# Edge messages with Wn2 padded to 128 columns, row groups for 20 quads, and edge attributes issued by ScalarE

## What is computed

```
gates    = (ssp(edge_state @ We1 + be1) @ We2 + be2) * soft_cutoff(distance)
h        = ssp(node_state[edges] (source and destination, 128 features) @ Wn1 + bn1) @ Wn2 + bn2
messages = h * gates
sums     = zeros.at[destination].add(messages)
x        = layernorm(x + x + ssp(sums @ Ws1 + bs1) @ Ws2 + bs2)
```

## Time and profile before

| | before |
|---|---|
| median of 3 runs | 1972.11 us (1970.78 to 1973.83) |
| the profiled execution | 1974.56 us, span 1972.8 us |
| mean granted clock of TensorE | 0.900 |
| PE / PEld / ACT busy | 1813.2 / 1389.2 / 1463.7 us |
| POOL / DVE busy | 1474.1 / 1233.8 us |
| HBM read and written | 139.69 and 9.87 MB |

### The profile page before, as it was taken

The page is one execution under the profiler, slowest core; times in us unless marked ns, Lnnn a source line. Parts: engine busy times, 40 slices in busy tenths (PEclk is TensorE's granted clock), DMA queues, the critical chain, the costliest instruction groups (busy, mean ns, idle before and its releaser), DMA issues.

```text
span 1972.8 us, 54212 instructions
## 1 busy us (share of the span) xinstructions
PE 1813.2 (92%) x16249; PEld 1389.2 (70%) x16249; DVE 1233.8 (63%) x3520; ACT 1463.7 (74%) x2593; POOL 1474.1 (75%) x1559
## 2 busy tenths in 40 slices
PE   3998998999999899989999999999999999999988
PEld 2777776777767677767777777777777666777766
DVE  4676765665756564655546666666667565566667
ACT  2586876775758676776768888888888777687877
POOL 7777777777777777777777777777777777777773
PEclk7598988896969896996869999999999998798999
DMA  6344434443444333343333334333333333333332
GB/s 125 77 82 93 94 82 90 79 86 76 82 76 71 76 70 64 70 71 69 67 64 80 78 75 80 76 75 81 73 82 74 72 75 73 68 75 76 72 72 45
DMA packets 238853, 151.26 MB, mean 77 GB/s; under 512 B 41936, under 2 KB 209822, under 8 KB 238746
## 3 DMA queue, kind: packets, MB, share of 16 engines
q0 software_dynamic: 49632, 50.87, 19.3%
q1 hardware_dynamic: 184773, 98.53, 18.6%
q10 hardware_dynamic: 4341, 0.72, 0.3%
HBM read 139.69 MB, written 9.87 MB: 76 GB/s over the span
## 4 chain that ended last, share of the span: by engine, by line
PE 43%; ACT 13%; SPq 13%; issue 11%; DMA 8%; DVE 6%; POOL 4%; DVEq 1%; ACTq 1%
PE ps L763 12%; PE ps L809 11%; PE ps L813 6%; SPq L409 5%; DMA ea<-in_edge_attr_dram 4%; PE ps L724 4%; POOL ga L549 4%; ACT lg L1121 3%; ACT lg L1116 3%; PE ps L701 3%; SPq L391 3%; PE ps L837 3%; DMA ga<-in_x_dram,srcT 2%; DVE hid L1413 2%; DVE hid L1417 2%
## 5 line engine op out<-in xcount | busy, mean ns | idle before, releaser
L549 POOL DMA_INDIRECT ga<-in_x_dram,srcT x1551 | 1473.1, 950 | 473.7 <-issue 437.1
L1108 ACT ACTIVATE lg<-ps,bn1c 128x512 f32<-128x512 f32 x390 | 267.9, 687 | 414.6 <-PE ps L724 409.5
L809 PE MATMUL ps<-wn,hid 128*128 128x64 f32 x3120 | 468.3, 297 | 56.4 <-DVE hid L1417 53.0
L809 PEld LDWEIGHTS ps<-wn,hid 128*128 128x128 f32 x3120 | 412.6, 206 | 90.6 <-DVE hid L1417 75.1
L1413 DVE SCALAR_TENSOR_TENSOR hid<-ps,neg_b,lg 128x512 f32<-128x512 f32 x390 | 292.0, 749 | 245.1 <-ACT lg L1121 240.2
L1116 ACT ACTIVATE lg<-lg 128x768 f32<-128x768 f32 x390 | 336.1, 862 | 0.0
L1121 ACT ACTIVATE lg<-lg 128x768 f32<-128x768 f32 x390 | 332.5, 852 | 0.0
L763 PE MATMUL ps<-xe,wn 64*128 64x256 f32 x1560 | 302.8, 468 | 0.5 <-DMA bw<-b_tab 0.5
L813 PE MATMUL ps<-we,hid 128*128 128x128 f32 x1560 | 284.8, 309 | 0.0
L1070 ACT COPY xe<-ps 128x512 f32<-128x512 f32 x390 | 229.4, 588 | 60.5 <-PE ps L703 59.6
L763 PE MATMUL ps<-ohT,bw 46*128 46x256 f32 x1560 | 259.5, 411 | 0.0
(11 more groups left out here) (173 smaller groups left out, 1634.7 us busy)
## 6 DMA issues: line engine op xcount, KB each, us to landing
ea<-in_edge_attr_dram SPq DMA_DIRECT2D x195, 256.0 KB
stage<-in_x_dram SPq DMA_DIRECT2D x1664, 0.2 KB
ga<-in_x_dram,srcT POOLq DMA_INDIRECT x1551
bw<-b_tab SPq DMA_DIRECT2D x782, 23.0 KB
relb<-rel_tab SPq DMA_DIRECT2D x196, 64.0 KB
b_tab<-share SPq DMA_DIRECT2D x24, 250.0 KB
out_dram<-xs SPq DMA_DIRECT2D x24, 125.0 KB
xs<-in_x_dram SPq DMA_DIRECT2D x5, 500.0 KB
```

Of the source, the lines that this page charges most:

```text
L549: pool.indirect_dma_start(to[:, t % 2, t // 2, :], None, x, bass.IndirectOffsetOnAxis(ap=idx[:, t:t + 1], axis=0)).then_inc(done, inc)
L809: pe.matmul(hg[:, t * D:(t + 1) * D], hid[:, u % 2, t * P:(t + 1) * P], wn2[:, :], start=False, stop=False, skip_group_check=True)
L1108: act.activation(lg[:, u % 2, 0:QUAD].rearrange("p (k e) -> p k e", k=2), z[:, :, 0:PAIR], ACT.Abs, bias=bn1c[:, 0:1])
```

## The change

Three edits. (1) Wn2 is kept in a tile of twice the width whose second half is zero (one more memset at the start). The matmuls of L809, and those of the last quad, move all 128 columns: 64 go to the messages' place of the PSUM bank, 64 zeros are added to the place of the gates. (2) The row quads are each 16th from quad 80, 20 in all; rows are fetched in turns of 16, one for each pair of quads from 22 quads ahead; PE waits for `handed` every 16th quad. (3) ea is issued by ACT: for quads 4 and 5 before its first step, then behind L1121 of each odd quad q for quads q+5 and q+6. The condition, that quad q+2 has been turned, is the same as on SP. SP loads ea for quads 0 to 3 alone.

```diff
-ROWS_EVERY = 24
-ROWS_N = 13
-ROWS_BEFORE = 30
-ROWS_TURN = (12, 8, 12, 12, 8, 12, 12, 8, 12, 12, 8, 12)
-HAND = 8
+ROWS_EVERY = 16
+ROWS_N = 20
+ROWS_BEFORE = 22
+ROWS_TURN = (16,) * 8
+HAND = 16
...
-        wn2 = sb("wn2", [P, D])
+        wn2w = sb("wn2w", [P, 2, D])
+        wn2 = wn2w[:, 0, :]
...
                 load_rel(q, u)
                 load_bw(q, v, firsts)
-                if reached(q, RING):
-                    load_ea(q, u)
                 load_rows(q)
                 hand_rows(q)
...
-                    pe.matmul(hg[:, t * D:(t + 1) * D], hid[:, u % 2, t * P:(t + 1) * P], wn2[:, :],
+                    pe.matmul(hg.rearrange("p (h t d) -> p t h d", h=2, t=4)[:, t, :, :], hid[:, u % 2, t * P:(t + 1) * P], wn2w[:, :, :],
                               start=False, stop=False, skip_group_check=True)
...
+            def load_ea(q, u):
+
+                act.wait_ge(xe_t, q - (RING - 2))
+                issue_ea(act, q, u)
+
             def fast_step(q, u, node=None, share_off=None):
                 if isinstance(q, int) and q == 0:
                     evacuate(0, 0)
                     evacuate(1, 1)
+                    load_ea(RING, 0)
...
                 logs(q, u)
+                if u % 2 == 1:
+                    load_ea(q + RING + 1, (u + 1) % RING)
...
                     logs(q, q % RING)
                     node_step(*node)
+                    if q % 2 == 1 and q + RING + 1 < NQ:
+                        load_ea(q + RING + 1, (q + 1) % RING)
...
+            dve.memset(wn2w[:, 1, :], 0.0)
```

More of the change, by code:

```diff
@@ L317, in general_of, with issue_ea @@
             return eng.value_load(flag_i[0:1, 0:1], min_val=0, max_val=1)
+        def issue_ea(eng, q, u):
+            if isinstance(q, int) and q == NQ - 1:
+                eng.dma_start(ea[0:LP, u, :, :],
+                              edge_attr[q * QUAD:E, :].rearrange("(k p j) d -> p k (j d)", k=2, j=2)).then_inc(s_ea[u], 16)
+            else:
+                two = edge_attr[bass.ds(q * QUAD, 2 * QUAD), :]
+                eng.dma_start(ea[:, u:u + 2, :, :].rearrange("p q k c -> p (q k) c"),
+                              two.rearrange("(m p j) d -> p m (j d)", p=P, j=2)).then_inc(s_ea[u], 16)
         LAST0 = PB // 15 * 15
@@ L368, in load_ea @@
                     sp.wait_ge(xe_t, q - (RING - 2))
[L369 to L375, removed]
+                issue_ea(sp, q, u)
             def load_rel(q, u):
@@ L794, in mid_last @@
                 for t in range(4):
-                    pe.matmul(hg[:, t * D:(t + 1) * D], hid[:, u % 2, t * P:t * P + LP], wn2[:, :],
+                    pe.matmul(hg.rearrange("p (h t d) -> p t h d", h=2, t=4)[:, t, :, :], hid[:, u % 2, t * P:t * P + LP], wn2w[:, :, :],
                               start=False, stop=False, skip_group_check=True)
```

## The result

| | before | after |
|---|---|---|
| median of the runs (us) | 1972.69 (1970.78 to 1977.28, 6 runs) | 2004.6 (1995.45 to 2016.93, 6 runs) |
| ratio, from all runs of both | | 1.0146, 95% interval 1.0119 to 1.0173 |
| profiled execution, its span (us) | 1974.56, 1972.8 | 1995.68, 1993.8 |
| granted clock, mean | 0.90 | 0.932 |

The forecast was 1966.6 us, with a range up to 1998. The kernel got 1.5% slower (the quotient of the two medians alone is 1.0162). The profiled execution is the second shortest of the six, 9 us under the median; all rows of "after" are of it.

The account below looks back on a forecast made before the run. POOL's gathers were taken to bound the kernel, before and after. Span 1972.8 - 7.5 (gathers removed) + 2 (ea's cost at the end) = 1967.3; the same 5.5 us off the median gave 1966.6 us, range 1961 to 1998.

Parts of the forecast that it names:

- What bounds the kernel before: Whole run: POOL's gathers, one each 1.25 us without a break, set the pace; PE catches up by about 1550 us.
- The gathers removed: POOL: 7 of 1551 gathers go, 6 of them up to quad 383, whose gather ends 7.5 us earlier.
- 128 columns: PE's Wn2 matmuls: 64 more columns cost 0 us and may raise the clock, credited with nothing.
- ea on ACT: ACT's queue: each ea issue takes 0.5 us, and PE's 45.5 us of waits for edge attributes should go.
- The +2 us at the end: ACT from quad 382 on: issuing ea and waiting behind quads 383 and 385 adds 2 us, from 0 to 3.
- SP's work for one pair: SP's issuing for two quads after the change: 9.25 to 9.5 us, under POOL's pace of 9.84 us.
- bw: SP's four window DMAs a pair: 1.48 us, with the long form of 2.64 us in one pair of five.
- the hold of 1.1 us: SP's first row behind ea: held up 1.1 us in the early part, taken to go when ea moves to ACT.
- The prediction's case for this, 10.3 us: SP's pair if the first row's 1.1 us delay stays with SP: 9.25 + 1.1 = 10.3 us, giving 2057 us.
- Windows' places: SP's load of eight windows' places every second pair: about 0.8 us each, half counted a pair as 0.45 us.
- Rows: SP's 16 single-row DMAs a pair, with register moves: 16 x 0.32 = 5.1 us.
- The rival's price: SP becomes the bound past 9.73 us a pair, each further 0.1 us costing 16 us: 1993 us, chance 0.22.

Follow-up runs that it names:

- E11: Changed kernel with 8 row DMAs a pair in place of 16, each bringing one row into two partitions: 1967.39 us, ratio 0.9956 to the kernel before.
- E10: Changed kernel with the row groups as before (13, every 24th quad), ea's move to ACT and 128 columns kept: 1975.07 us, ratio 0.9988 to before.
- E12: Changed kernel with a row group at every 20th quad, 16 in all: 1971.56 us, ratio 0.9981 to the kernel before.
- E13: Changed kernel with the 64 columns of before in the messages' second layer: 2002.28 us, ratio 1.0118 to the kernel before.
- E16: Kernel before with windows of 48 rows in its bw DMAs and nothing of the change: 1971.21 us, ratio 0.9970 to the kernel before.
- E15: Changed kernel with windows of 48 rows in place of 46 in the bw DMAs, the two more unused: 1966.13 us, ratio 0.9951 to before.
- E14: Changed kernel with relb fetched by two DMAs of 64 partitions in place of one of 128: 1990.84 us, ratio 1.0073 to the kernel before.
- E17: Changed kernel with both windows of 48 rows and relb in two DMAs of 64 partitions: 2046.14 us, ratio 1.0344 to the kernel before.
- E9: The changed kernel itself, run again without further edits: 2009.95 us, ratio 1.0145 to the kernel before.
- E18: Changed kernel with windows of 48 rows in the bw DMAs, run once more: 1967.7 us, ratio 0.9944 to the kernel before.
- E1: On a slower chip, the changed kernel with the 13 row groups of before: 2496.89 us, ratio 0.9787 to the kernel before there.
- E8: On a slower chip, the changed kernel with 16 row groups, every 20th quad: 2526.59 us, ratio 0.9795 to the kernel before there.
- E6: On a slower chip, the changed kernel with half of SP's row DMAs: 2499.96 us, ratio 0.9701 to the kernel before there.
- E3: On a slower chip, the kernel before with only the 128 columns added: 2496.75 us, ratio 0.9785 to the kernel before there.
- E5: On a slower chip, the changed kernel with 64 columns again: 2626.41 us, ratio 1.0183 to the kernel before there.

## Why the prediction was wrong, by its own steps

**What bounds the kernel before: right.** With the row groups' load off SP the time follows POOL's gathers, 1.25 us each: 6 fewer before quad 383 are 7.7 us (E11 against E10), 3 fewer 3.9 (E12).

**The gathers removed: right** as a gain that is there if SP is. E11 gives it without anything else changed but SP's issues.

**128 columns: right.** No time, more clock (0.90 to 0.93), and no credit taken for it (E10, E13).

**ea on ACT: right in effect.** Its issue is short, and PE's waits for ea went from 45.5 us to none:

```profile
L327 ACTq DMA_DIRECT2D ea<-in_edge_attr_dram x193: 374/379/407, 50.3 to 1952.9; - x193
```

The +2 us at the end can't be told from nothing: E10's median is 1.2 us over before's, its ratio 0.1% under 1, with an interval from -0.4% to +0.1%.

**SP's work for one pair: this is where it failed.** The forecast had 9.25 to 9.5 us and POOL as the bound at 9.84; SP takes about 10.0 with its stops between 1000 and 1800 us and 10.06 over all turns, and is the bound. It failed in four terms.

*bw.* The forecast took the short form, 1.48 us, with the long one in one pair of five. It is 2.07 on the mean, and 2.3 in the first 20 pairs: 0.36 us a pair over the mean form, the largest part of what was lacking. The long form was in the trace of before (2.64 in the earlier trace rows), and the hold of 1.1 us behind ea too. I asked only whether the hold belonged to SP's queue or to the DMA engines, answered "SP's queue" from the start's rows, and took it as gone with ea. ACT's ea is never held (at most 407 ns, above), and moving ea did free the first row. But the hold stayed with SP whole. Before, between 1000 and 1800 us, the first row of a turn takes 547 ns on the mean and 44 of 86 take over 500; in E10, with the same row groups, it is 330 ns and 6 of 80. In the same stretch bw's mean rises from 340 to 430 ns, and 4 x 0.09 is 0.36 us a pair (before, then E10):

```profile
L391 SPq DMA_DIRECT2D bw<-b_tab x344: 237/251/2504, 1003.3 to 1795.8; - x172
```

```profile
L396 SPq DMA_DIRECT2D bw<-b_tab x320: 238/254/1596, 1008.1 to 1793.5; - x160
```

It was relb's and bw's, not ea's: E16 takes it away with ea in its place, E15 and E14 with ea gone. The prediction's case for this, 10.3 us, had the mechanism nearly right and the size wrong, since its 1.1 us was read off one turn.

*Windows' places.* The 0.8 us for each is the median of all (787 ns), and not that of the early part, where SP's load waits behind other traffic: the load of L479 between 310 and 531 us in the kernel before, and L484 in the changed one (ns min/median/max):

```profile
L479 SPq TENSOR_LOAD <-wb_all x11: 1635/2141/3632, 313.0 to 525.8; - x11
```

```profile
L484 SPq TENSOR_LOAD <-wb_all x10: 1243/2154/3523, 316.0 to 514.2; - x10
```

2.17 against 0.79 us on the mean is 0.7 us a pair for the first 20 pairs, in which SP also stores 10 shares (0.3 us each, not in my sum). These pairs take 11.04 us, and 20 x (11.04 - 10.06) = 20 us of SP's reserve are gone by 531 us. E15 has nearly the same (10.74) and is in time, so this term alone doesn't make the loss. A window of the trace from this part would have shown it; the prediction took one steady pair for all 160.

*Rows.* 5.29 against 5.1, since a pair's last gap and the first rows behind bw (0.27 in place of 0.23) were not in it.

*Stops.* 0.12 us a pair, 20 us over 160 pairs, for which the sum had no term.

**The rival's price: right in slope, wrong in where it starts.** The slope was 16 us for each 0.1 us a pair; E17 against E15 gives 15. The limit was put at 9.73 us a pair, on the argument that the last turn must start by 1869 us. By the last line of each turn's row DMAs, the ends are (first and last start; the spans are 1993.8, 2014.1, 2001.2, 1964.0 and 2047.5 for the changed kernel, E9, E13, E15 and E17):

```profile
L414 SPq DMA_DIRECT2D stage<-in_x_dram x2560: 224/228/532, 310.1 to 1915.0; - x197
```

```profile
L414 SPq DMA_DIRECT2D stage<-in_x_dram x2560: 224/228/855, 311.1 to 1933.5; - x197
```

```profile
L414 SPq DMA_DIRECT2D stage<-in_x_dram x2560: 224/228/882, 306.8 to 1919.9; - x197
```

```profile
L415 SPq DMA_DIRECT2D stage<-in_x_dram x2560: 224/228/347, 303.8 to 1885.3; - x197
```

```profile
L416 SPq DMA_DIRECT2D stage<-in_x_dram x2560: 227/228/594, 304.7 to 1971.0; - x197
```

Span less last start is 78.8, 80.6, 81.3, 78.7 and 76.5 us, in E14 and E18 80.2 and 83.7: wherever SP is the bound, the end follows its last row by 76 to 84 us. Where POOL is, it is more (E11: 96.7). The prediction allowed 1967.3 - 1869 = 98 us from the start of the last turn, its load of the places, to the end, and its last row starts 6.2 us behind that: 92. The first turn's first row is at 304 us in E15, too, where the prediction had its load at 322. E15 brings the forecast's time with a mean pair of (1880.4 - 303.8) / 159 = 9.92 us, and E11, in which SP waits 514.5 us for ohT, ends no earlier; so the limit is at about 9.92 and not 9.73. The changed kernel needs 10.06 and starts 6 us later: 159 x 0.147 + 6.3 = 29.7 us, and its span is 29.8 over E15's. That the prediction's 9.9 us a pair gave 1993, near the profiled 1995.7, was luck, two errors that cancelled: 9.9 would just have been in time, and the pair was 10.06.

**The chances.** 0.22 for SP was too little for a reserve of 0.3 us in 9.7 whose largest uncertain term, the hold, was as large as 1.1. The Trainium skill's rule that was weighed there (DMA: Bandwidth & Descriptors, "Issuing engines are not separate DMA queues") says that issuing from another engine saves the sequencer's time of issuing alone. E10's bw agrees with it in that the hold of 0.3 to 0.4 us a pair stayed, and it deserved more weight; but the hold wasn't ea's.

## What to carry to other kernels

When work is put on an engine that only issues, sum all that it does for one round, from a window of each phase of the run, and not from one clean round; the reserve of 5% in the forecast was none here. A DMA issue that takes several times its shortest time may be held by what was queued before it: find what that is, since moving the held instruction only handed the hold on here. And count DMA engines before bytes: by the rule cited above 46 rows go to two of them and 48 to 16, and the version with two rows that nobody needs was 2% faster here (1.0146 to 0.9951).

Of what was run, the change with windows of 48 rows is the fastest: 0.9951 (0.9932 to 0.9971) and 0.9944 (0.9924 to 0.9965) of before. relb as one DMA over 16 engines with bw at 46 rows would make a pair of about 9.3 us, an estimate by E14's 9.89 less the second issue of 0.57; it wasn't tried.

## What the runs showed of the hardware that was not expected

**The price of a DMA issue on SP follows its shape.** 0.228 us for a row of 256 bytes, 0.251 for 46 partitions of 512 bytes (E14), 0.372 for 48 partitions (E15), 0.54 for relb, all medians.

**SP stops after every 128 instructions**, for 0.35 to 0.38 us, in the changed kernel between 1000 and 1800 us, 26 times of 26. What it does then was not looked into; each instruction on SP costs some 3 ns by this beside its own time (0.37 / 128, an estimate).

**Two chips where the engines wait longer.** On the chips of E1 to E8 ACT's and DVE's instructions take the time that they take elsewhere, but the idle time between them is longer, and much of it is put down to "remote", which is to say that the profile finds no releaser on this core. ACT's first Abs, E6 and then E11 (busy, mean ns, idle before, releaser), the same kernel on both:

```profile
L1113 ACT ACTIVATE lg<-ps,bn1c 128x512 f32<-128x512 f32 x390 | 267.8, 687 | 970.2 <-remote 902.1
```

```profile
L1113 ACT ACTIVATE lg<-ps,bn1c 128x512 f32<-128x512 f32 x390 | 267.6, 686 | 342.9 <-PE ps L729 339.6
```

687 against 686 ns of work, 970 against 343 us of idle time before it. POOL isn't full there: it waits 523 us for "remote" in E6, and makes 257 gathers between 1100 and 1500 us where it made 320. That the loop goes round over PE, ACT and DVE there, and that PE's clock counts for that reason (E3), fits this but is not shown. SP's own instructions show the like. E5's register moves in front of the row DMAs, then those of E13, the same kernel:

```profile
L414 SPq MOVE stage<-in_x_dram x2560: 2/29/1400, 440.6 to 2529.3; - x197
```

```profile
L414 SPq MOVE stage<-in_x_dram x2560: 29/29/38, 306.7 to 1919.9; - x197
```

A register move of 29 ns is recorded with 2 ns to 1.4 us. Single durations can't be trusted there, with a shortest of 2 ns; but a row with its move takes 0.54 us on the mean of E5's (1000 to 1800 us) where it takes 0.33. What makes these two chips so was not found; the runs without a profile were as long, and every kernel showed it.
